# Two GpSimd transfers of eight partitions per DMA engine for the tails of a store

## What is computed

```
x = x + conv(group_norm(x), weight, bias)
# group_norm: 16 groups of 2 channels, mean and variance over both channels and all rows
# conv: ifft(einsum(fft(x padded), fft(w padded))), rows and columns 64 to 191 of 256, plus bias
```

## Time and profile before

| | |
|---|---|
| median of 3 runs | 82.82 us |
| lowest, highest | 82.75, 83.03 us |
| the profiled execution | 82.75 us, of which the span is 81.5 us |
| TensorE busy | 67.7 us |
| VectorE, ScalarE, GpSimd busy | 50.2, 48.0, 31.6 us |
| DMA over the span | 33.62 MB, 412 GB/s |

### The profile page before, as it was taken

The page is one execution under the profiler, slowest core; times in us unless marked ns, Lnnn a source line. Parts: engine busy times, 40 slices in busy tenths (PEclk is TensorE's granted clock), DMA queues, the critical chain, the costliest instruction groups (busy, mean ns, idle before and its releaser), DMA issues.

```text
span 81.5 us, 684 instructions
## 1 busy us (share of the span) xinstructions
PE 67.7 (83%) x222; PEld 41.8 (51%) x222; DVE 50.2 (62%) x43; ACT 48.0 (59%) x53; POOL 31.6 (39%) x43
## 2 busy tenths in 40 slices
PE   0019865999999999999999999999999999999000
PEld 0014424556666666666666666666666665665000
DVE  0019936960399779949994996899499735100700
ACT  3308958980299669947974994799299553000000
POOL 6994000004029950000999690086029206800000
PEclk9999995557999999999999999999999999999998
DMA  1999999999979997799597997979969999988976
GB/s 21 336 434 438 458 426 408 457 461 466 482 338 466 399 608 336 336 608 399 238 546 337 490 490 279 529 305 514 498 289 466 418 402 466 480 382 382 525 325 253
DMA packets 2020, 33.62 MB, mean 412 GB/s; under 512 B 280, under 2 KB 314, under 8 KB 484
## 3 DMA queue, kind: packets, MB, share of 16 engines
q1 hardware_dynamic: 1876, 33.36, 96.1%
q0 software_dynamic: 96, 0.19, 0.7%
q10 hardware_dynamic: 48, 0.06, 0.3%
HBM read 16.84 MB, written 16.78 MB: 412 GB/s over the span
## 4 chain that ended last, share of the span: by engine, by line
PE 77%; DMA 14%; DVE 2%; SPq 1%; issue 0%; POOL 0%; POOLq 0%
PE ps L437 75%; DMA images<-x_dram 14%; DVE images L453 2%; PE ps_m L339 1%; SPq L195 1%; PE ps_w L285 1%; POOL pair L233 0%; POOL eps L199 0%; POOLq L605 0%
## 5 line engine op out<-in xcount | busy, mean ns | idle before, releaser
L437 PE MATMUL ps<-g,w_sb 128*128 128x363 f32 (+1 forms) x192 | 61.9, 480 | 0.0
L437 PEld LDWEIGHTS ps<-g,w_sb 128*128 128x128 f32 x192 | 36.6, 197 | 20.5 <-issue 2.3
L418 POOL TENSOR_SCALAR images<-images,bias_sb 128x1984 f32<-128x1984 f32 (+3 forms) x12 | 23.2, 1941 | 26.9 <-ACT origin L313 18.4
L303 DVE TENSOR_REDUCE sums<-images 128x1 f32<-128x4096 f32 x7 | 30.9, 4411 | 0.6 <-DMA images<-x_dram 0.6
L324 ACT ACTIVATE unused<-images,origin 128x4096 f32<-128x4096 f32 (+1 forms) x9 | 30.0, 3331 | 0.3
L453 DVE SCALAR_TENSOR_TENSOR images<-ps,bias_sb,images 128x1089 f32<-128x1089 f32 (+2 forms) x9 | 10.9, 1221 | 7.7 <-PE ps L437 7.7
L394 ACT ACTIVATE g<-images,rstd 128x1089 f32<-128x1089 f32 (+2 forms) x8 | 9.4, 1192 | 3.4 <-DVE rstd L368 3.4
L303 DVE TENSOR_REDUCE first_sums<-images 128x1 f32<-128x2048 f32 x2 | 4.6, 2286 | 5.9 <-DMA images<-x_dram 5.9
L356 DVE TENSOR_SCALAR var<-ps_m,square 128x1 f32<-128x1 f32 x8 | 1.7, 218 | 9.4 <-ACT square L351 9.4
L351 ACT ACTIVATE square<-ps_m,origin 128x1 f32<-128x1 f32 x8 | 2.1, 262 | 8.4 <-PE ps_m L339 8.4
L285 PE MATMUL ps_w<-images,avg 128*128 128x1 f32 x4 | 1.1, 355 | 6.9 <-POOL bias_sb L499 5.9
(11 more groups left out here) (21 smaller groups left out, 13.0 us busy)
## 6 DMA issues: line engine op xcount, KB each, us to landing
images<-x_dram SPq DMA_DIRECT2D x1, 5344.0 KB, 36.8
images<-x_dram SPq DMA_DIRECT2D x1, 4096.0 KB, 24.6
out_dram<-images SPq DMA_DIRECT2D x1, 4096.0 KB
out_dram<-images SPq DMA_DIRECT2D x2, 2048.0 KB
out_dram<-images SPq DMA_DIRECT2D x1, 3904.0 KB
out_dram<-images SPq DMA_DIRECT2D x1, 3040.0 KB
images<-x_dram SPq DMA_DIRECT2D x1, 2080.0 KB, 15.5
images<-x_dram SPq DMA_DIRECT2D x2, 1024.0 KB, 5.8
```

What stands on the lines that cost most here:

```text
L303: lambda e: e.tensor_reduce(to_sum(img, k)[:, 0:1], piece, mybir.AxisListType.X, ALU.add),
L418: "pool", lambda e: e.tensor_scalar(part, part, 1.0, bias_sb, op0=ALU.mult, op1=ALU.add),
L437: lambda e, k=k, dc=dc, rows=rows, top=top: e.matmul(ps[:, 0:rows, 0 : N - dc], w_sb[:, k * P : (k + 1) * P], g[:, top : top + rows, dc:N] ...
```

## The change

The tails of the first pair are divided in another way.

- SyncE's small store takes partitions 32 to 47 (16 tails) in place of 126 and 127.
- GpSimd stores the other 112 tails by two transfers: partitions 48 to 127 as 10 steps of 8 rows, and partitions 0 to 31 as 4 steps of 8 rows. Source partition 8a + b of a part goes to row 10b + a (or 4b + a) of it, and the host puts them back.
- `take_first` for image 6 waits for the sixth load alone, no longer for the seventh. It reads row 0 of the image, which the sixth load brings.

```diff
-    MOST = 126
+    SPREAD = slice(32, 48)
+    GROUP = 8
...
-            *rows_in(img, H if img == B - 2 else 1), *needs, *([group_ok[img - 3]] if img > 3 else []), mark=True,
+            *rows_in(img, 1), *needs, *([group_ok[img - 3]] if img > 3 else []), mark=True,
...
-                store(flat(out[0])[MOST:P, most:], flat(pairs[0])[MOST:P, most:], *finished(0, 1))
+                store(flat(out[0])[SPREAD, most:], flat(pairs[0])[SPREAD, most:], *finished(0, 1))
...
-                    spread = flat(out[0])[0:MOST, most:].rearrange("(b a) n -> a b n", b=3)
-                    moved = store(spread, flat(pairs[0])[0:MOST, most:], *biased[1], turned, by="pool")
+                    for part in (slice(SPREAD.stop, P), slice(0, SPREAD.start)):
+                        to = flat(out[0])[part, most:].rearrange("(b a) n -> a b n", b=GROUP)
+                        moved = store(to, flat(pairs[0])[part, most:], *biased[1], turned, by="pool")
...
-    last = out[0, :126, 1, -6:]
-    last[:] = last.reshape(3, 42, *last.shape[1:]).transpose(1, 0, 2, 3).reshape(last.shape)
+    for part in (slice(48, P), slice(0, 32)):
+        last = out[0, part, 1, -6:]
+        last[:] = last.reshape(8, -1, *last.shape[1:]).transpose(1, 0, 2, 3).reshape(last.shape)
```

## The result

| | before | changed |
|---|---|---|
| median (22 runs each) | 82.87 us | 83.13 us |
| lowest, highest | 82.74, 83.03 | 82.95, 83.50 |
| the profiled execution, and its span | 82.75, 81.5 us | 83.07, 81.8 us |

The ratio is 1.0028, with a 95% interval of 1.0019 to 1.0037: 0.26 us slower. The forecast was 0.15 us faster.

The account below looks back on a forecast made before the run. The fullest DMA engine was taken to set the end. Half the excess (-0.13) and a third of the balance term (-0.02) gave -0.15 us: 82.75 to 82.60, plus 0.07 for the median, 82.67 us; range 82.40 to 83.00.

Parts of the forecast that it names:

- The bound: At the last store: the fullest DMA engine sets the end, the compute path being ready at least 0.24 us earlier.
- The engines' side: GpSimd's second issue (0.69 us more) and the dropped wait on the seventh load are hidden: cost nothing.
- half the excess, -0.13: DMA queues, 48 to 54 us: tails cost 0.26 us per engine beyond their bytes; half of that goes, -0.13 us.
- nothing but balance: Second rival, DMA queues: the excess stays and only balance is left, 82.76 to 82.95 us; chance 0.22.
- priced on GpSimd only: GpSimd's second transfer of tails: its issue is covered by idle time before the bias step, so it costs nothing.
- priced at its bytes: SyncE's 16-row store in the balance term: one tail more for each engine, 57 ns per tail.
- The third rival: SyncE's queue: the small store through all 16 engines leaves a gap, up to 0.85 us; 83.2 at 0.4 us; chance 0.08.
- The balance term: Tails per DMA engine divided more evenly: -0.06 to +0.06 us, of which a third, -0.02 us, was taken.
- 14 large ones: GpSimd's queue, 48 to 54 us: 14 packets of eight tails in place of 42, one per outer step.
- the first two rivals: DMA queues: all the excess goes, 82.3 to 82.55 us, chance 0.20; or only balance is left, 82.76 to 82.95, chance 0.22.
- the slow one: The third rival's case, a gap in SyncE's queue: 83.1 us and above, chance 0.08.

Follow-up runs that it names:

- wait_only: The kernel before with only the change's new wait (the copy for image 6 waits for the sixth load alone): 1.0008 of before.
- The twins: quads_turn16 and quads_turn8: all tails by four GpSimd transfers, differing only in the rows of a tiny load ahead (16 or 8): 1.0138 and 1.0243 of before.
- own_one: Against before: one plain GpSimd transfer of all 128 tails without a scatter, no small SyncE store: 1.0069 of before.
- no_small: The changed kernel without SyncE's small store, so the 16 tails of partitions 32 to 47 are not stored: 1.0025 of before.
- eights_only: Against before: one GpSimd transfer of partitions 0 to 111 as 14 steps of 8 rows; no small store, other 16 tails not stored: 1.0002.
- eights_one: Against before: one GpSimd transfer of partitions 0 to 111 as 14 steps of 8 rows; SyncE stores the 16 tails of partitions 112 to 127: 1.0025.
- eights_late: eights_one with SyncE's 16-row small store issued later, after the store of images 2 and 3: 1.0015 of before.
- all_sync: Against before: no transfer of tails; SyncE's store of images 0 and 1 takes whole partitions and GpSimd stores nothing: 1.0024.
- nines_one: Against before, with the new wait: one GpSimd transfer of the same 126 tails as 14 steps of 9 rows in place of 42 of 3: 1.0002.
- quads_turn16: Against before: all 128 tails by four GpSimd transfers of 8 steps of 4 rows, no small store, tiny load ahead of 16 rows for 6: 1.0138.
- quads_turn8: quads_turn16 with 8 rows in place of 16 in the tiny load ahead of the transfers: 1.0243 of before.
- nines_two: nines_one with the 126 tails split over two GpSimd transfers, 90 as 10 steps of 9, then 36 as 4 steps of 9: 1.0124 of before.
- nines_swapped: nines_two with the small transfer first: 36 tails as 4 steps of 9, then 90 as 10 steps: 1.0036 of before.

## Why the prediction was wrong

- **The bound was right.** DMA engines set the end: with the compute path 0.6 us earlier the end came 0.3 us later, which says it more strongly than the issue times did.
- **The engines' side was right.** GpSimd's two issues took 1.20 us, not 1.38, and left 0.28 us of idle time before the bias step; the removed wait moved nothing (wait_only). The profile of the changed kernel, GpSimd near 44 us:

```profile
43.55 1.20 POOL L463 DMA_DIRECT2D out_dram<-images  x2
44.75 0.31 POOL L279 COPY sums<-images 128x1 f32<-128x1 f32 x2
45.34 3.03 POOL L419 TENSOR_SCALAR images<-images,bias_sb 128x1984 f32<-128x1984 f32 x2 [0.28 <-ACT origin L314]
```

- **The step that failed is "half the excess, -0.13".** It took the change's word that eights are the engines' own partitions and gave the effect one sign. The excess did not fall by 0.13 us per engine, it rose by 0.21. The twins and own_one show that the cause named is real: who reads a partition changes the stretch (61 ns a tail in own_one, 73 and 115 in the twins). But the change's tails took 98 ns, so it doesn't provide such readers. The rule of the Trainium skill that said so stood in the prediction, with the chance of "nothing but balance"; its consequence was read as zero, where it should have been read as "unknown, and of either sign".
- **The second transfer was priced on GpSimd only.** As an issue it is free. In the DMA queues the kernel with two transfers and no small rows is 0.2 us slower than the one with a single transfer (no_small and eights_only, 1.0025 and 1.0002). That it is the split, by the burst, and not the other readers that may come with it, is argued and not shown.
- **The small store was priced at its bytes, one tail for each engine.** The third rival saw that it now passes through all 16 engines, but as a gap in the queue, at 0.4 us. There is no such gap: without that store the change is only 0.03 us faster (no_small, 1.0025). Beside one GpSimd transfer it costs 0.1 to 0.2 us, by the ratios of eights_one and eights_late against eights_only, whose intervals overlap.
- **The balance term** (+-0.06 us) is too small to be seen in any run here. It took all engines to be equally fast, and all_sync shows that with an even division one ends 0.6 us behind the others.
- **The packets.** 14 large ones were forecast; in 48 to 54 us there are 42 between 2 and 8 KB (176 less 134), as many as in before. So eight tails travel as 3, 3 and 2, and an engine's tails are not in one piece. nines_one, with 14 steps, also has 42 (84 less 42), so the prediction's reading of one packet per step of the outer dimension was wrong too.
- The range ended at 83.00. It was bounded by the first two rivals, and the slow one got 0.08: two additions to the queues with no row of their own (a second transfer, 16 small rows) deserved a bound above zero. The measured 83.13 us lies in the slow case (83.1 and above), but by luck: the cause given there, a gap in SyncE's queue, isn't what happened.

## What to carry to other kernels

Where the DMA engines set the end, price a store by who reads which partition and by what runs beside it, not by bytes alone: the same tails cost from 61 to 115 ns each here. One more transfer, or one more row for each engine, may be hidden on the issuing engine, as both were here, and still cost some 0.2 us in the queues. Before evening out an uneven division, look whether an engine that it spares is slower than the rest.

## What the hardware showed that was not expected

- With equal bytes on all 16 DMA engines, one of them ends behind the others at the end of the stores: after 81.10 us it alone still had a data packet to start, in four kernels. In all_sync it fell behind between 52 and 72 us and by 0.6 us.
- Four GpSimd stores cost some 0.4 to 0.7 us outside the span: 83.67 us for a span of 82.0 us in quads_turn16, 84.83 for 83.1 in quads_turn8, against 1.2 to 1.3 us outside in the others.
- Rows of one engine that lie 14 rows apart in HBM are no dearer than three near each other (1.0002).
- The order of two transfers that hold the same tails changed the time by 0.9% (nines_two and nines_swapped), and in the slower order four engines end behind the other twelve.
